# Post-norm attention and int8 linear layer on one core: the order of the last batch's requests, of the seam between batches, and of the splits of v and of the tokens

## The chip, the cores and the metric

The kernel runs on one core of one Trainium2 chip. The metric is the time of one execution on the device in microseconds (us); the time before is the median of three runs. A profile of one execution gives the times of instructions, from the start of its span.

## The reference

X has 4 batches of 1024 tokens with 512 features. With `q = X Wq` (16 heads of 64), `k = X Wk` and `v = X Wv` (8 heads of 64, each for two heads of q), and rotary embedding on q and k:

```
att = softmax(causal(50 * tanh(q k^T / 16 / 50)))
x   = layernorm(X + (att v) Wo)
q8, s = per-token int8 of x          # s = max(absmax, 1e-7) / 127, q8 = clip(round(x / s))
f   = float16((q8 @ weight^T) * s * w_scale + bias)
out = layernorm(x + f)
```

## The kernel before

Every float32 product is made of three products of rounded parts: high x high, high x low, low x high. ScalarE makes a high part by copying into the rounded type, VectorE or GpSimd (POOL) makes the low part by subtraction. The five engines each have an instruction list of their own, written out by hand, and wait for each other through semaphores. All loads, and the stores of intermediate results, are asked for by the queue SP in one order; the output stores are asked for by ScalarE's queue.

**A batch** (`b`) has 4 units (`u`), each for two heads of k and four of q, and a unit has 18 steps (`s`). Step `g = 18 u + s` treats one tile of 128 x 1024 scores:

- TensorE makes the scores (`score`), and three steps later (`LAG`) weighs v with the probabilities (`weigh`).
- ScalarE makes tanh (`cap`, the squashing) and exp (`exponent`). POOL sets the part over the diagonal to zero in the steps that have one (`mask`, one select or two). VectorE makes high and low parts (`probs_of`, which waits for the mask; `low_done` lets `weigh` go).
- ScalarE copies finished sums (`keep_sums`), and SP stores them to `y_scratch` (`put_sums`). The last row of the sums holds the softmax denominators.

**Beside the scores** a unit makes q and k of the next one, in three chunks (`x` = 0 for k, 1 and 2 for the halves of q). A chunk is 24 products of TensorE in three slices of 8 (`project`), a rotation on VectorE (`rope_read`, for k four operations of 1024 columns), a rounding on ScalarE (`round_rope`), a low part on VectorE (`rope_low`), and a spreading into `qk` by transfers (`put`: 4 for k, 8 for a half of q). `turns` says at which steps of the unit these run: its result for unit 3 is the list of steps moved by 2, 1 and 1. The chunks of unit 3 belong to the next batch, whose tokens are split in four parts (`split_x`, on ScalarE and VectorE) at the steps that `part_at` names. They are also what SP's loads of w_v, the weights of v, wait for.

**After the steps** TensorE makes v for the next batch (`project_v`), beside the inverses of the denominators. SP loads a group's denominators (`load_div`), VectorE inverts them (`invert`), SP stores the inverses (`store_inverse`) and loads them as rows (`load_rows`), TensorE spreads the rows over the partitions (`spread_rows`), and VectorE scales y with them (`scale_y`), which `load_y` has loaded. `round_y` and `split_y` (ScalarE, POOL) make its parts.

**Then come the 8 row tiles** (`t`) of 128 tokens: `project_out` (24 products with Wo), `residual1` (waits for X in `x_in`), `inverse_std`, `shift_by` and `norm1` for the first norm, `find_scale` and `quantise`, `turn_q` (4 transposes) with its copy `keep_q`, `linear`, `rescale`, `residual2` (two additions on POOL: bias, then the row), `stats2`, `inverse_std`, `shift_by`, `norm2` and `store` for the second. `inverse_std` of a tile waits for the norm of the one before. The tiles pass through rings: `ffn_tile` lies in the same buffer as the probabilities, and `done_tile` puts the last two tiles' output into `x_in`.

**The seam** is the end of a batch's tiles, in which the next batch's first steps have begun: scores 0 and 1 are made between the last tiles, the squashings of 0, 1 and 2 stand between the last norms, and that of 3 waits until the last norm is done, since tiles 6 and 7 lie in the buffer that it writes. In the last batch nothing follows, and the tiles run without work beside them.

**The start** makes v 0 to 7, the tables and the three chunks of unit 0. `round_v` and `split_v` make the high and low part of a tile of v; the first projection of unit 1 waits for all low parts of v and for `proj_read`.

## Time and profile before

| | |
|---|---|
| median of 3 runs | 1356.7 us (1356.2 to 1359.26) |
| the profiled execution | 1350.54 us |
| its span, first to last instruction | 1348.8 us |
| mean granted TensorE clock | 0.983 of full |
| TensorE busy | 1277.5 us, 95% |
| VectorE busy | 1041.9 us, 77% |
| ScalarE busy | 898.6 us, 67% |
| POOL busy | 392.6 us, 29% |

The span is measured within the profiled execution, whose own time lies 1.7 us above it. A batch takes about 327 us, so what is seen in batch 1 comes again in the next one some 327 us later. PE is TensorE, DVE is VectorE, ACT is ScalarE, and SPq is the request queue. L724 is line 724 of the kernel. A wait for several semaphores is put down to the one that came last, and "issue" means that the profile shows no releaser.

### The profile page before, as it was taken

How to read it: one execution, taken by the hardware profiler on the slowest of the kernel's cores; microseconds unless marked ns; L12 is line 12 of the kernel's file. 1: busy time of each engine (PE TensorE's matmuls, PEld its weight loads, DVE VectorE, ACT ScalarE, POOL GpSimd, SP SyncE). 2: the span in 40 equal slices, each digit the busy share in tenths (PEclk: the TensorE clock that was granted, in tenths of full speed). 3: DMA queues.
4: the chain of work that ended last, by engine and by line, in shares of the span. 5: the costliest groups of instructions: out<-in, count | busy, mean ns of one | idle time of the engine just before them, and what ended most of it. 6: DMA issues, size and time to landing. Idle time of an engine off the chain costs nothing.

```text
span 1348.8 us, 17012 instructions
## 1 busy us (share of the span) xinstructions
PE 1277.5 (95%) x5840; PEld 940.1 (70%) x5840; DVE 1041.9 (77%) x1300; ACT 898.6 (67%) x1017; POOL 392.6 (29%) x454
## 2 busy tenths in 40 slices
PE   7899999999989999999998999999999899999795
PEld 5677776767757777677775777767776677777473
DVE  4598998874778888986579888888567888888565
ACT  4378778663667777865466867787346687779354
POOL 4232221112751121111383211121157211111266
PEclk9899999999999999999999999999999999999897
DMA  8784647394715364658632644548662445353641
GB/s 312 172 254 117 150 107 197 89 256 144 176 60 134 83 163 98 176 116 259 158 103 63 168 94 120 114 152 214 194 171 83 91 128 111 87 120 111 169 111 55
DMA packets 112403, 191.46 MB, mean 142 GB/s; under 512 B 19382, under 2 KB 65980, under 8 KB 104764
## 3 DMA queue, kind: packets, MB, share of 16 engines
q1 hardware_dynamic: 107708, 181.97, 51.4%
q10 hardware_dynamic: 4608, 8.39, 1.7%
q8 instruction: 47, 0.77, 0.2%
q14 instruction: 40, 0.33, 0.1%
HBM read 84.67 MB, written 38.54 MB: 91 GB/s over the span
## 4 chain that ended last, share of the span: by engine, by line
PE 84%; DVE 6%; issue 3%; ACT 2%; POOL 2%; DMA 1%; SPq 1%; ACTq 0%; POOLq 0%; DVEq 0%
PE ps L804 26%; PE ps L724 18%; PE ps L778 17%; PE ps L848 12%; PE ps L745 6%; PE ps L868 1%; DVE prob_hi L1221 1%; PE ps L824 1%; DVE xT L1162 1%; DMA y_scratch<-sums 1%; ACT probs L998 1%; POOL rstd L1445 1%; DVE stats L1301 1%; POOL f L1454 0%; PE ps L858 0%
## 5 line engine op out<-in xcount | busy, mean ns | idle before, releaser
L804 PE MATMUL ps<-prob_hi,v 128*65 128x512 f32 (+3 forms) x1280 | 412.6, 372 | 4.5 <-DVE prob_lo L1225 4.2
L998 ACT ACTIVATE probs<-ps 128x1024 f32<-128x1024 f32 x288 | 293.6, 1019 | 149.2 <-PE ps L778 146.2
L1225 DVE TENSOR_TENSOR prob_lo<-probs,prob_hi 128x1024 fp32r<-128x1024 f32 x288 | 363.9, 1264 | 9.9
L1430 POOL TENSOR_SCALAR_AFFINE_SELECT probs<-probs 128x256 f32<-128x256 f32 (+1 forms) x192 | 154.9, 814 | 724.1 <-ACT probs L1003 724.1
L778 PE MATMUL ps<-qk 128*128 128x512 f32 (+1 forms) x1280 | 315.3, 373 | 14.7 <-ACT probs L998 13.0
L1003 ACT ACTIVATE probs<-probs 128x1024 f32<-128x1024 f32 x288 | 305.7, 1061 | 9.8 <-ACT probs L1047 1.2
L724 PE MATMUL ps<-xT,w_ring 128*128 128x512 f32 x1152 | 289.9, 395 | 11.0 <-DVE xT L1162 6.1
L1221 DVE CAST prob_hi<-probs 128x1024 fp32r<-128x1024 f32 x288 | 212.6, 738 | 90.9 <-POOL probs L1430 53.4
L778 PEld LDWEIGHTS ps<-qk 128*128 128x128 f32 x1280 | 225.5, 189 | 74.3 <-ACT probs L998 15.6
L724 PEld LDWEIGHTS ps<-xT,w_ring 128*128 128x128 f32 x1152 | 217.1, 190 | 58.9 <-DVE xT L1162 7.4
L804 PE MATMUL ps<-prob_lo,v 128*65 128x512 f32 (+1 forms) x640 | 237.8, 372 | 0.0
L804 PEld LDWEIGHTS ps<-prob_hi,v 128*65 128x65 f32 (+1 forms) x1280 | 171.6, 135 | 94.2 <-DVE prob_lo L1225 8.9
L848 PE MATMUL ps<-wo,y_hi 128*128 128x512 f32 x512 | 132.4, 402 | 1.3 <-POOL y_lo L1436 1.3
L804 PEld LDWEIGHTS ps<-prob_lo,v 128*65 128x65 f32 x640 | 87.1, 136 | 50.1 <-issue 0.4
L848 PEld LDWEIGHTS ps<-wo,y_hi 128*128 128x128 f32 x512 | 95.7, 191 | 29.7 <-issue 9.1
L1019 ACT ACTIVATE sums<-ps 65x512 f32<-65x512 f32 x128 | 74.5, 582 | 59.7 <-PE ps L804 59.7
L745 PE MATMUL ps<-w_v,xT 128*128 128x512 f32 x384 | 93.5, 400 | 10.2 <-DVE w_v L1316 8.1
L1436 POOL TENSOR_TENSOR y_lo<-y_raw,y_hi 128x1024 fp32r<-128x1024 f32 x32 | 76.5, 2391 | 90.1 <-ACT y_hi L1027 89.7
L745 PEld LDWEIGHTS ps<-w_v,xT 128*128 128x128 f32 x384 | 72.7, 192 | 29.1 <-issue 12.0
L848 PE MATMUL ps<-wo,y_lo 128*128 128x512 f32 x256 | 67.8, 389 | 0.0
L981 ACT ACTIVATE work_r<-work 128x1024 fp32r<-128x1024 f32 x48 | 50.1, 1044 | 18.6 <-DVE work L1201 10.6
L1207 DVE TENSOR_TENSOR work_r<-work,work_r 128x1024 fp32r<-128x1024 f32 x48 | 58.5, 1219 | 2.8 <-ACT work_r L981 2.8
(86 smaller groups left out, 967.1 us busy)
## 6 DMA issues: line engine op xcount, KB each, us to landing
qk<-work_r SPq DMA_DIRECT2D x64, 512.0 KB, 8.8
qk<-work_r SPq DMA_DIRECT2D x256, 128.0 KB, 2.7
y_scratch<-sums SPq DMA_DIRECT2D x128, 130.0 KB
wo<-wo_scratch SPq DMA_DIRECT2D x8, 2048.0 KB, 7.9
y_raw<-y_scratch SPq DMA_DIRECT2D x64, 256.0 KB, 4.2
w_ring<-w_scratch SPq DMA_DIRECT2D x12, 1024.0 KB, 6.8
x_raw<-X_T SPq DMA_DIRECT2D x16, 512.0 KB, 6.2
x_in<-X SPq DMA_DIRECT2D x32, 256.0 KB, 4.1
```

The source lines that it names most:

```text
L724: mm = nc.tensor.matmul(ps[:, bank + n, :], w_ring[:, slot, w, k, :], xT[:, a, k, half * HT:(half + 1) * HT], start=(k == w == a == 0), st ...
L745: mm = nc.tensor.matmul(ps[:, v_bank(b, t), :], xT[:, a, k, t * P:(t + 1) * P], weights[:, w, k, :], start=(k == a == w == 0), stop=(k == ...
L778: mm = nc.tensor.matmul(scores[:, g % 2, col:col + REP * w].rearrange("p (h q) -> p h q", h=REP), qk[:, n % 2, i, 3 - part, keys], qk[:, n ...
L804: mm = nc.tensor.matmul(sums_ps[:, :, GQ - w:GQ], v[:, kt, v0:v0 + width], p[:, at, col:col + REP * w].rearrange("p (h q) -> p h q", h=REP ...
L848: mm = nc.tensor.matmul(bank, (y_lo[:, y_place(t), k, :] if a else y_hi[t % 2][:, k, :]), wo[:, w, k, :], start=(n == 0), stop=(n == 3 * K ...
L998: nc.scalar.activation(probs[:, prob_place(g), :], scores[:, g % 2, :], ACT.Tanh, scale=SCORE_SCALE / SOFTCAP).then_inc(capped, 1)
L1003: nc.scalar.activation(probs[:, prob_place(g), :], probs[:, prob_place(g), :], ACT.Exp, scale=SOFTCAP).then_inc(exped, 1)
L1019: nc.scalar.activation(sums[0:VJ, slot, :], ps[0:VJ, PV_BANK + c % 2, :], ACT.Copy).then_inc(sums_kept, 1)
L1221: nc.vector.tensor_copy(prob_hi[:, hi_place(g), :], probs[:, prob_place(g), :]).then_inc(rounded, 1)
L1225: nc.vector.tensor_tensor(prob_lo[:, prob_place(g), :], probs[:, prob_place(g), :], prob_hi[:, hi_place(g), :].bitcast(F32), ALU.subtract) ...
L1430: nc.gpsimd.affine_select(out=diag, in_=diag, compare_op=ALU.is_ge, fill=0.0, base=0, pattern=[[0, n], [1, P]], channel_multiplier=-1).the ...
L1436: nc.gpsimd.tensor_tensor(y_lo[:, y_place(t), :, :], y_raw[:, y_place(t), :, :], y_hi[t % 2][:, :, :].bitcast(F32), ALU.subtract).then_inc ...
```

## The change

- **Start.** v tiles 6 and 7 are rounded and split sooner: ScalarE rounds them ahead of the rounding of chunk 2, and VectorE splits tile 6 ahead of that chunk's rotation and tile 7 ahead of its low part. The first projection of unit 1 no longer waits for `proj_read`.
- **Chunks.** In unit 3 the chunks run 3, 2 and 2 steps later than listed, not 2, 1 and 1; in unit 0 of every batch but the first they run one step later; the third chunk's rounding, low part and spreading stand one step sooner in the lists (so in units 1 and 2 they come a step sooner). The last token split moves from step 0 to step 1 of unit 3.
- **Seam.** Tiles 6 and 7 lie in `x_in` from the rescaling on, so the squashing of score 3 waits only for the stores of tiles 3 and 4. ScalarE does the squashings and exponentials of scores 1 to 3 ahead of the norm of tile 7, which moves with its store behind step 4, and copies the last quantised tile ahead of the exponential of score 1. VectorE rescales tile 7 ahead of the statistics of tile 6, makes probabilities 1 ahead of tile 6's shift, and makes tile 7's shift behind probabilities 2.
- **Last batch.** Inverse 0 is made and stored one step sooner. y 2, then the denominators of group 2, then rows 2 are asked for ahead of the last sums, and rows 3 right behind them; X still comes after. The first `project_out` begins with the products of high parts. The last quantised tile is copied ahead of a norm and its store, and VectorE makes the second residual of the last tile.

```diff
         def ffn_tile(t):
-            return blocks[:, FFN_BLOCK[t % FRING], :]
-        def done_tile(t):
-            return x_in[:, t % XRING, :] if t >= NT - 2 else ffn_tile(t)
+            return x_in[:, t % XRING, :] if t >= NT - 2 else blocks[:, FFN_BLOCK[t % FRING], :]
-        def turns(u, *steps):
-            return tuple(s + (2, 1, 1)[x] for x, s in enumerate(steps)) if u == UB - 1 else steps
+        def turns(b, u, *steps):
+            return tuple(s + (3, 2, 2)[x] for x, s in enumerate(steps)) if u == UB - 1 else \
+                tuple(s + 1 for s in steps) if b >= 1 and u == 0 else steps
-            return {(2, 15): 0, (2, 16): 1, (2, 17): 2, (3, 0): 3}.get((u, s))
+            return {(2, 15): 0, (2, 16): 1, (2, 17): 2, (3, 1): 3}.get((u, s))
 # SP
-                        if at := chunk_at(b, u, s, turns(u, 6, 11, 15)):
+                        if at := chunk_at(b, u, s, turns(b, u, 6, 11, 14)):
                             put(sp, *at)
+                        if (b, u, s) == (B - 1, UB - 1, 16):
+                            store_inverse(b, 0)
                         if u == UB - 1 and s == 17:
-                            if b + 1 == B:
-                                store_inverse(b, 0)
                             load_div(b, 1)
...
                 put_sums(b, NKV - 1, G - 2)
-                load_div(b, 2)
-                put_sums(b, NKV - 1, G - 1)
-                load_div(b, 3)
-                load_y(b, 2)
+                if b + 1 < B:
+                    load_div(b, 2)
+                    put_sums(b, NKV - 1, G - 1)
+                    load_div(b, 3)
+                    load_y(b, 2)
+                else:
+                    load_y(b, 2)
+                    load_div(b, 2)
+                    load_rows(b, 2)
+                    put_sums(b, NKV - 1, G - 1)
+                    load_rows(b, 3)
+                    load_div(b, 3)
                 for t in range(XRING):
                     load_x(b, t)
-                load_rows(b, 2)
-                load_rows(b, 3)
+                if b + 1 < B:
+                    load_rows(b, 2)
+                    load_rows(b, 3)
 # TensorE
-                    if m > 0:
+                    if m > 1 or x > 0 and m > 0:
                         pe.wait_ge(proj_read, chunks_upto(m, x) - 1)
-                products.sort(key=lambda p: p[1] if t else p[2])
-                if lo == (2 * KO if t else 0):
+                products.sort(key=lambda p: p[1] if t else (p[2], p[1]))
+                if lo == (2 * KO if t else KO):
                     pe.wait_ge(y_lo_done, rows_upto(b, t))
 # ScalarE
                     if g == 3:
-                        act.wait_ge(normed, rows_upto(b - 1, NT - 1))
+                        for t in (NT - 5, NT - 4):
+                            act.wait_ge(out_stored[t % FRING], stores_upto(b - 1, t))
...
-            round_rope(0, 2)
             round_v(0, 6)
             round_v(0, 7)
+            round_rope(0, 2)
...
+                        if b >= 1 and g == 4:
+                            norm2(b - 1, NT - 1)
+                            store(b - 1, NT - 1)
...
                 if more:
                     cap(b + 1, 1)
-                norm2(b, NT - 3)
+                    norm2(b, NT - 3)
+                keep_q(b, NT - 1)
+                if not more:
+                    norm2(b, NT - 3)
                 store(b, NT - 3)
                 if more:
                     exponent(b + 1, 1)
-                keep_q(b, NT - 1)
+                    cap(b + 1, 2)
+                    exponent(b + 1, 2)
                 norm2(b, NT - 2)
                 store(b, NT - 2)
                 if more:
-                    cap(b + 1, 2)
-                    exponent(b + 1, 2)
-                norm2(b, NT - 1)
-                store(b, NT - 1)
+                    cap(b + 1, 3)
+                    exponent(b + 1, 3)
+                else:
+                    norm2(b, NT - 1)
+                    store(b, NT - 1)
 # VectorE
+            def residual2(b, t):
+                dve.wait_ge(scaled, rows_upto(b, t))
+                dve.wait_ge(bias_loaded, bias_upto(b))
+                dve.wait_ge(x2_done, rows_upto(b, t - 1))
+                nc.vector.tensor_tensor(f16[:, :], ffn_tile(t), bias[:, :], ALU.add).then_inc(biased, 1)
+                dve.wait_ge(biased, rows_upto(b, t))
+                nc.vector.tensor_tensor(ffn_tile(t), f16[:, :], row_tile(t), ALU.add).then_inc(x2_done, 1)
...
             split_v(0, 5)
+            split_v(0, 6)
             rope_read(0, 2)
+            split_v(0, 7)
             rope_low(0, 2)
-            split_v(0, 6)
-            split_v(0, 7)
...
-                        if (b, u, s) == (B - 1, UB - 1, 16):
+                        if (b, u, s) == (B - 1, UB - 1, 15):
                             invert(b, 0)
                         if g >= 1 and not at_end(b, u, s - 1):
                             probs_of(b, g - 1)
+                        if b >= 1 and g == 3:
+                            shift_by(b - 1, NT - 1, 1, rstd2, shift2)
...
                 shift_by(b, NT - 3, 1, rstd2, shift2)
                 if more:
                     probs_of(b + 1, 0)
-                stats2(b, NT - 2)
+                if not more:
+                    stats2(b, NT - 2)
                 rescale(b, NT - 1)
+                if more:
+                    stats2(b, NT - 2)
+                else:
+                    residual2(b, NT - 1)
+                if more:
+                    probs_of(b + 1, 1)
                 shift_by(b, NT - 2, 1, rstd2, shift2)
-                if more:
-                    probs_of(b + 1, 1)
                 stats2(b, NT - 1)
-                shift_by(b, NT - 1, 1, rstd2, shift2)
+                if not more:
+                    shift_by(b, NT - 1, 1, rstd2, shift2)
 # POOL
                 residual2(b, NT - 2)
+                if b + 1 < B:
+                    mask(b + 1, 1)
                 inverse_std(b, NT - 2, 1, mv2, veps2, rstd2, normed)
                 if b + 1 < B:
-                    mask(b + 1, 1)
-                residual2(b, NT - 1)
+                    residual2(b, NT - 1)
                 inverse_std(b, NT - 1, 1, mv2, veps2, rstd2, normed)
```

The lists of the other engines for a chunk change alike: TensorE `turns(b, u, 0, 5, 9)`, VectorE's rotation `(b, u, 3, 8, 12)`, ScalarE's rounding `(b, u, 5, 10, 14)` becomes `(b, u, 5, 10, 13)`, VectorE's low part `(6, 11, 15)` becomes `(6, 11, 14)`. `mask` of score 1 does nothing, since that tile has no diagonal.

## Rows read from the trace of the kernel before

**Rows 1.** Waits of TensorE over the span: us in total, times, longest.

```profile
PE ps L778 <- ACT probs L998: 13.0, 6, 2.8
```

**Rows 2.** Timeline at the start: start, us, engine, line, out<-in, count, idle before.

```profile
54.98 0.68 DVE L1201 TENSOR_TENSOR work<-work 128x512 f32<-128x512 f32 x1
...
57.93 1.28 DVE L1167 TENSOR_TENSOR v<-ps,v 128x512 fp32r<-128x512 f32 x2
58.04 5.81 SPq L457 DMA_DIRECT2D qk<-work_r  x8
...
59.31 3.75 PE L724 MATMUL ps<-xT,w_ring 128*128 128x512 f32 x8 [4.39 <-issue]
...
66.25 1.07 PE L778 MATMUL ps<-qk 128*128 128x512 f32 x4
```

**Rows 3.** Chain that ended last, in order of time: start, us, what.

```profile
64.56 1.85 PE ps L724 x8
...
1238.56 1.39 PE ps L804 x6
1239.94 0.92 PE ps L778 x4
```

**Rows 4.** The page's transfer requests: count, KB each, median us to landing.

```profile
qk<-work_r SPq DMA_DIRECT2D x256, 128.0 KB, 2.7
...
result<-probs ACTq DMA_DIRECT2D x24, 256.0 KB, 2.3
```

**Rows 5.** Timelines around three waits: seam one, unit 3, seam two.

```profile
294.93 2.96 PE L745 MATMUL ps<-w_v,xT 128*128 128x512 f32 x12 [1.00 <-issue]
...
564.59 1.06 ACT L1003 ACTIVATE probs<-probs 128x1024 f32<-128x1024 f32 x1
...
567.73 2.11 PE L724 MATMUL ps<-xT,w_ring 128*128 128x512 f32 x8 [2.03 <-DVE xT L1162]
...
621.65 2.90 PE L745 MATMUL ps<-w_v,xT 128*128 128x512 f32 x12
```

**Rows 6.** The w_v requests ahead of seam two: issue times, landing.

```profile
L557 SPq DMA_DIRECT2D w_v<-wv_scratch x2: 442/442/443, 614.5 to 615.0; - x2
...
DMA to landing us min/median/max: 4.6/5.5/6.4
```

**Rows 7.** Timeline of seam one.

```profile
393.25 2.06 DVE L1225 TENSOR_TENSOR prob_lo<-probs,prob_hi 128x1024 fp32r<-128x1024 f32 x1
...
397.11 0.41 POOL L1430 TENSOR_SCALAR_AFFINE_SELECT probs<-probs 128x256 f32<-128x256 f32 x1
...
397.36 1.23 DVE L1186 TENSOR_TENSOR work<-ps,cosT 128x1024 f32<-128x1024 f32 x1
...
405.02 1.23 DVE L1225 TENSOR_TENSOR prob_lo<-probs,prob_hi 128x1024 fp32r<-128x1024 f32 x1
...
408.42 0.39 PE L804 MATMUL ps<-prob_hi,v 128*65 128x512 f32 x1
```

**Rows 8.** Timeline of the last batch's first tiles.

```profile
1267.17 0.32 SPq L487 DMA_DIRECT2D div<-y_scratch  x1
...
1271.19 1.08 SPq L472 DMA_DIRECT2D x_in<-X  x2
...
1275.37 0.69 DVE L1257 TENSOR_TENSOR probs<-ps,x_in 128x512 f32<-128x512 f32 x1 [5.72 <-DMA x_in<-X]
...
1276.67 1.19 PE L824 MATMUL ps<-rows,spread 4*128 4x512 f32 x2 [6.88 <-DMA rows<-r_scratch]
...
1281.35 0.72 ACT L1043 ACTIVATE q<-probs,round_down 128x512 bf16<-128x512 f32 x1
...
1286.63 3.94 PE L848 MATMUL ps<-wo,y_hi 128*128 128x512 f32 x16
```

**Rows 9.** Timeline of the end.

```profile
1339.90 0.75 DVE L1293 SCALAR_TENSOR_TENSOR probs<-ps,in_scale,w_scale 128x512 f32<-128x512 f32 x1 [0.57 <-PE ps L868]
...
1343.26 0.69 DVE L1301 BATCH_NORM_STATS2 stats<-probs 128x6 f32<-128x512 f32 x1 [2.49 <-POOL probs L1456]
```

More of the change, by code:

```diff
@@ L916, in _ @@
                         spread_rows(b, t + 1)
[L917 to L918 removed]
+                    for third in range(3):
+                        project_out(b, t, third * KO, (third + 1) * KO)
                     if t >= 2:
```

20 lines of the change are left out of this document (9 added, 11 removed).

## The prediction

> **What bounds the kernel now.** I read the page first, then the waits of TensorE, then the timeline around each wait, and the transfer queue where a wait ended on a transfer. TensorE is busy for nearly the whole span (the table above), so time can only be won where it stands idle or runs at the low clock. Its longest waits are for ScalarE's squashing at the three seams between batches, 13.0 us [rows 1]; the others fall at the start, before unit 3, in the last batch and at the end, and are taken one by one below. Inside the units it hardly waits. So I take the edits place by place, and ask each time which wait ends last afterwards.
>
> **Start: v split sooner.** The first projection of unit 1 starts at 59.31 after 4.39 us of idling [rows 2]. By the code it waits for all eight low parts of v. VectorE makes the last two from 57.93, 0.64 us each, because ScalarE rounds v 6 and 7 only after a rotation result that VectorE finishes at 54.98 + 0.68 = 55.66 [rows 2]. With the new order v 6 fits into VectorE's wait ahead of that rotation, and v 7 runs at 55.7 to 56.35. The projection may start at 56.4, 2.9 us sooner. What is late next is the second half of q: its eight requests run from 58.04 for 5.81 us, which does not move, since it needs the rotation's rounding; the score at 66.25 needs four of them. The fourth is issued at 58.04 + 3 x 0.73 = 60.2 and lands 2.7 us later, 62.9 [rows 2, 4]. That leaves room for 66.25 - 62.9 = 3.3 us, so the 2.9 holds. Bounds: 1.5 (requests landing later, as TensorE's idling moves there) and 3.3. I take 2.9 won.
>
> **Token splits and shifted chunks.** In each of the first three batches the first chunk of unit 3 waits 2.03 us, until 567.73 in batch 1, for the last token split [rows 5]. The split moves one step later, the chunk too. A step without projection is one score and one weighing, 1.39 + 0.92 = 2.3 us of TensorE [rows 3]. On ScalarE the exponential of unit 3's first step, done at 564.59 + 1.06 = 565.65 [rows 5], no longer stands behind the split and ends about 0.9 us sooner. Its mask is two selects of some 0.4 to 0.5 us, as the one of 0.41 [rows 7], and VectorE then has 2.0 us of probabilities and 1.2 us of split (a subtraction as wide as the 1.23 of rows 7). Exponential done 564.75, mask 565.9, probabilities 567.9, split 569.15. Without the shift TensorE would have started the same chunk after the same work at 567.73 + 2.3 = 570.0. Won: 0.8 per batch, 2.4 in all. Bounds: 0 (the mask slowed to twice its time by VectorE beside it) and the 2.03 x 3 = 6.1 of the waits.
>
> The same shift costs at the end of unit 3. There the queue asks for the second half of w_v right behind the requests of the middle chunk, which now come one step later. In the first seam TensorE already waits 1.00 us at 294.93 for v's first product. In the second the requests went at 614.5 and 615.0 and the later landed after 6.4 us, at 621.4, against a start of 621.65 [rows 5, 6]: no slack. A whole step is 2.3 us, but the sums of group 0 (0.6 us of queue) now go ahead of the chunk's requests, and VectorE does the chunk's low half before the next rotation and not behind it; I take 1.1. That is 1.1 lost in seam one, 1.1 - 0.25 = 0.85 in seam two, and I count nothing for seam three, where v's product started without a wait too (the 0.85 there is in the bounds): 2.0 lost. Bounds: 0 and 2.3 x 3 = 6.9. The other chunk edits (last third rounded a step sooner; unit 0 a step later) lie under TensorE's full stretches; without that cover each costs at most one rounding, about 1 us.
>
> **The seam.** The squashings of scores 1 to 3 go ahead of the last norms, so the 13.0 us of waits for them [rows 1] go. But VectorE is late next. In the old order it starts the rotation at 397.36, and ends the low half of probabilities 3 at 405.02 + 1.23 = 406.25, with almost no gap. TensorE weighs them at 408.42 [rows 7]. The rotation is four operations of 1.23, so it ended at 402.3, and a pair of probabilities takes (406.25 - 402.3) / 2 = 2.0. In the new order VectorE first does probabilities 2. Their mask ran at 397.11 to 397.52 behind POOL's last inverse deviation; POOL's order keeps that, and the statistics of tile 7 that it needs still come behind probabilities 1. So: mask 397.5, probabilities 2 to 399.5, rotation to 404.4, probabilities 3 to 406.4. TensorE has one slice of projection (1.85 us [rows 3]) less ahead of weighing 3, since unit 0's middle chunk is a step later: like for like it got there at 408.42 - 1.85 = 406.57. New against old, 406.4 to 406.57: nothing won. The waits for squashings turn into waits for probabilities and for the rotation. Bounds: 1.9 us either way per seam, about that pair, which the ordering may put outside or inside the chain. I take 0, since both sides of the sum are made of rows.
>
> Here a rule weighs against the change. Beside POOL's additions the low half at 393.25 took 2.06 us against 1.23 [rows 7]: the two engines slow each other. The Trainium skill, SBUF — State Buffer, section Who interferes with whom, says that VectorE with two inputs in SBUF and GpSimd contend, and that the one that starts first holds the shared ports for its whole instruction. The trace agrees that they contend; what holding would do here is rival (b).
>
> **Last batch.** TensorE idles 6.88 us until 1276.67 for rows 2. They were asked for behind y 2 and two tiles of X, and those behind a second pair of transfers for the sums. Now y 2, the inverses and the rows follow the first pair, which lands by 1267.17 [rows 8]; the rows' requests go at about 1267.6. Only y 2 is ahead of them, so they land at about 1270, and the second product block runs from 1271 to 1276.7. The next wait is then the first quantised tile. Its residual started at 1275.37, after 5.72 us of waiting for X, and it was complete at 1281.35 + 0.72 = 1282.07, 6.7 later [rows 8]. X is still asked for last, at about 1270.8. At 1271.19, behind y, it took 4.2 us [rows 8]; a store of the same size with nothing ahead takes 2.3 [rows 4]; I take 3.0, so 1273.8, 1.5 sooner, and the tile is ready at 1280.6. TensorE idles 3.9 us for it and comes back at the low clock, as at 59.31, where eight products after 4.39 us of idling took 3.75 against 1.85 us [rows 2, 3]: 1.9 us more, or 2.2 with the transposes ahead. The third block, at 1286.63 before [rows 8], starts at 1280.6 + 1.0 = 1281.6 behind turning and spreading: 5.0 us sooner, less 2.2: 2.8 won. Bounds: 1.5 (X hardly sooner) and 5.0 (clock kept). Inverses 0 gain little: their store now waits for the queue's four y requests, 0.25 us sooner than before. The first product's new order lets it start sooner, but the rows of tile 2 end that stretch.
>
> **Tail.** ScalarE copied the last quantised tile behind a norm and its store; it now comes ahead of them, about 1 us sooner. But the rescaling, at 1339.90 with 0.57 us of idling ahead, can move up only by these 0.57, as the statistics of tile 6 stand ahead. VectorE then adds bias and row itself: 2 x 0.69 (as the addition at 1275.37 [rows 8]) plus about 0.3 for waits and one shift, 1.7, where POOL's two took from 1340.65 to 1343.26, 2.6 [rows 9]. Won 0.55 + 0.9 = 1.45. Bounds: 0.6 and 2.
>
> **Sum.** -2.9 - 2.4 + 2.0 + 0 - 2.8 - 1.45 = -7.5 us. The profiled execution took 1350.54, so 1343.0 for the same; the median of the timed runs is 1356.7, 6.2 above it, and I set the difference against that: 1349.2. No change by measurement means within 0.2%, 2.7 us.
>
> **Rivals.** (a) The seams do give: VectorE's chain shortens by the 1.9 us each, or TensorE keeps its clock in the last batch. For it: VectorE has idle time there beside POOL. Against it: 406.25 is reached with hardly a gap. Gain 7.5 + 5.7 = 13.2 from the seams alone: 1343.5.
>
> (b) The ports decide. Probabilities 1 run against POOL's additions for tile 7; if POOL is held for both of VectorE's operations, 1.9 us per seam, its mask and all behind it are that much late: -7.5 + 5.8 = -1.7, 1355: no change. For it 2.06 against 1.23 [rows 7]; against it, the same pair met before. The rule of the first starter, in the Trainium skill, SBUF — State Buffer, section Who interferes with whom, would give just this if VectorE starts first.
>
> (c) Slower: the new knot on ScalarE. Squashing 2 now waits for the store of tile 5 and stands ahead of norm 6, which POOL's last deviation and so mask 2 wait for. Squashing and exponential take 2.1 us; with the store landing in the usual 2.3 us [rows 4] they end, as I count the order, some 3 us before norm 6 could start anyway, since its shift stands behind probabilities 1, whose low half ended at 395.31 before [rows 7]. It makes the kernel slower by over 0.2% from (7.5 + 2.7) / 3 = 3.4 us per seam beyond those 3, a landing of 8.7 us. The longest of the rows is 6.4 [rows 6]. Reached, it would give 1360.
>
> (d) The moves do not do what they say: the rows still land behind y and X, and w_v costs its full 6.9. Then -7.5 + 1.3 + 4.9 = -1.3: 1355.4.
>
> **How the numbers follow.** Forecast 0.56, (a) 0.22, (b) 0.08, (d) 0.08, (c) 0.06. The forecast's own range, from its bounds taken half together, is 1345 to 1353.5. With (a), half of (b) and (d), 8 in 10: 1342.5 to 1355.5. Faster: the forecast nearly whole and (a), with a little of the others, 0.83; same 0.11; slower 0.06.
>
> **What would show it.** Right: unit 1's first projection near 56.4; the chunk wait of unit 3 under 1.7 us; waits for ScalarE's squashings nearly gone and waits for VectorE's probabilities or rotation in their place; v's first product in seams one and two waiting about 2 and 0.8 us; rows 2 landing near 1270 on the old clock, with a wait for the quantised tile behind the second block; the end 1.4 us shorter behind the last product block. Wrong: seams shorter by over 1 us each, or TensorE at full clock after the wait in the last batch, would make it faster than I say; waits for w_v over 3 us, or a landing of tile 5's store that shows in squashing 2, slower.

## The result, and the profile after

The change makes the kernel slower: 1362.5 us (median of 6 runs, 1360.2 to 1363.8) against 1356.5 (6 runs beside them), ratio 1.0049 with a 95% interval of 1.0029 to 1.0069, 4 to 9 us. The prediction was 1349.2, faster.

The profiled execution took 1363.67 us, its span is 1361.9, and the granted clock 0.982 as before. The spans differ by 13.1 us and the medians by 6: the profiled execution of before lies 6 us under its median, this one 1 us above. So the traces tell where time goes, and the timed ratios how much.

Waits of TensorE over the span after: us in total, times, longest.

```profile
PE ps L813 <- DVE prob_lo L1243: 22.2, 24, 3.0
PE ps L867 <- ACT q L1053: 9.1, 5, 5.1
...
PE ps L787 <- ACT probs L1008: 5.6, 4, 1.4
PE ps L754 <- issue: 4.9, 3, 2.4
PE ps L733 <- DVE xT L1180: 4.4, 3, 1.5
PE ps L787 <- DMA qk<-work_r: 2.8, 1, 2.8
...
PE ps L833 <- DMA rows<-r_scratch: 1.6, 1, 1.6
```

The same view of the kernel before, for VectorE's low parts of probabilities:

```profile
PE ps L804 <- DVE prob_lo L1225: 4.2, 7, 0.8
```

The 13.0 us for squashings [rows 1] are 5.6 now, but three waits stand there that were small or absent: those low parts (22.2, before 4.2), q's transfer at the start (2.8, before none), and v's first product (L754, "issue": 4.9, before 1.0).

The start, TensorE's timeline:

```profile
56.59 2.09 PE L733 MATMUL ps<-xT,w_ring 128*128 128x512 f32 x8 [1.43 <-issue]
...
64.24 2.06 PE L787 MATMUL ps<-qk 128*128 128x512 f32 x4 [2.84 <-DMA qk<-work_r]
66.10 2.76 PE L733 MATMUL ps<-xT,w_ring 128*128 128x512 f32 x8
```

The projection came 2.7 us sooner, as said. This time TensorE kept the clock behind its wait (eight products in 2.09 us, against 3.75 [rows 2]), so it came to the score at 61.40 already. It waited 2.84 us for q, until 64.24 and not 62.9, and came back at the low clock: four products of the score took 2.06 us, against 1.07 [rows 2]. At the start of unit 1 (116 us) 0.3 us of the lead was left.

Unit 3 of batch 1, which answers to the 2.03 us wait of [rows 5]: POOL's selects in the kernel before (L1430), then, in the changed one, the same selects, the last split and the chunk.

```profile
565.82 2.35 POOL L1430 TENSOR_SCALAR_AFFINE_SELECT probs<-probs 128x256 f32<-128x256 f32 x2 [2.43 <-ACT probs L1003]
...
569.26 1.95 POOL L1465 TENSOR_SCALAR_AFFINE_SELECT probs<-probs 128x256 f32<-128x256 f32 x2 [1.84 <-ACT probs L1013]
...
573.12 1.22 DVE L1180 TENSOR_TENSOR xT<-x_raw,xT 128x1024 fp32r<-128x1024 f32 x1
...
574.39 2.11 PE L733 MATMUL ps<-xT,w_ring 128*128 128x512 f32 x8 [1.46 <-DVE xT L1180]
```

The end of unit 3, batch 0, on the queue and on ScalarE, and v's first product behind it:

```profile
268.53 7.42 SPq L450 DMA_DIRECT2D qk<-work_r  x4
275.99 1.95 SPq L650 DMA_DIRECT2D wo<-wo_scratch  x1
277.98 3.01 SPq L569 DMA_DIRECT2D y_scratch<-sums  x2
283.23 6.85 SPq L457 DMA_DIRECT2D qk<-work_r  x8
290.18 0.54 SPq L487 DMA_DIRECT2D div<-y_scratch  x1
290.82 0.87 SPq L557 DMA_DIRECT2D w_v<-wv_scratch  x2
...
289.90 0.59 ACT L1029 ACTIVATE sums<-ps 65x512 f32<-65x512 f32 x1 [2.67 <-DMA y_scratch<-sums]
...
297.29 0.94 PE L754 MATMUL ps<-w_v,xT 128*128 128x512 f32 x3 [0.20 <-issue]
...
629.57 4.29 PE L754 MATMUL ps<-w_v,xT 128*128 128x512 f32 x12 [2.26 <-issue]
...
963.43 2.97 PE L754 MATMUL ps<-w_v,xT 128*128 128x512 f32 x12 [2.44 <-issue]
```

The last two lines are v's first twelve products at the ends of batches 1 and 2. At the end of batch 0 the first starts 2.4 us later than before (294.93). w_v's second half was asked for at 290.82, where before it was at 287.16: it stands behind the middle chunk's eight requests, which start a step later, and now behind the denominators' request too, which keeps its fixed step 14. Beside this, ScalarE waits 2.67 us to copy sums: the buffer's last store, asked for right behind wo's 2 MB, took until then to land. In the trace's own chain of what ended last, batch 0 goes through that store:

```profile
277.98 11.84 DMA y_scratch<-sums
```

So TensorE waits only 0.20 us for w_v there; ahead of seams two and three it waits 2.26 and 2.44 us (1.00, 0 and 0 before). Behind the 2.26 the clock fell too: v's first twelve products took 4.29 us, against 2.90 [rows 5], and behind the 2.44 it did not (2.97).

Seam one, VectorE and TensorE (L1319 statistics, L1239 and L1243 probabilities, L1204 rotation):

```profile
398.48 0.69 DVE L1319 BATCH_NORM_STATS2 stats<-x_in 128x6 f32<-128x512 f32 x1 [2.29 <-POOL x_in L1491]
...
400.81 0.69 DVE L1239 CAST prob_hi<-probs 128x1024 fp32r<-128x1024 f32 x1 [1.31 <-POOL probs L1465]
...
402.81 1.22 DVE L1204 TENSOR_TENSOR work<-ps,cosT 128x1024 f32<-128x1024 f32 x1
...
402.82 0.69 PE L813 MATMUL ps<-prob_hi,v 128*65 128x512 f32 x1 [3.01 <-DVE prob_lo L1243]
...
410.12 0.45 PE L813 MATMUL ps<-prob_hi,v 128*65 128x512 f32 x1 [1.29 <-DVE prob_lo L1243]
```

TensorE waits 3.01 us in one piece and comes back at the low clock (0.69 us for a product that takes 0.39).

The last batch, queue, VectorE and TensorE; all is 16.5 us later than before:

```profile
1284.10 0.56 SPq L503 DMA_DIRECT2D rows<-r_scratch  x2
...
1287.54 1.84 SPq L472 DMA_DIRECT2D x_in<-X  x2
...
1286.45 0.73 PE L833 MATMUL ps<-rows,spread 4*128 4x512 f32 x2
...
1297.91 0.61 PE L867 MATMUL ps<-ident,q 128*128 128x128 bf16 x4 [5.09 <-ACT q L1053]
...
1299.60 5.67 PE L857 MATMUL ps<-wo,y_hi 128*128 128x512 f32 x16
...
1291.24 0.69 DVE L1275 TENSOR_TENSOR probs<-ps,x_in 128x512 f32<-128x512 f32 x1 [4.56 <-DMA x_in<-X]
```

Rows 2 are spread 6.7 us sooner than before, like for like (1286.45 - 16.5 against 1276.67 [rows 8]); X is only 0.6 us sooner (its residual at 1291.24 - 16.5 = 1274.7 against 1275.37). The new wait for the quantised tile, 5.09 us, costs the clock: the next 16 products take 5.67 us, against 3.94 [rows 8].

**Where the difference arises.** The start of ScalarE's squashing at the same step, after less before (us):

| batch, unit, step | before at | after | chunks_only | seam_only | seam_rotation |
|---|---|---|---|---|---|
| 0, 3, 14 | 284.26 | 0.85 | 0.58 | -0.15 | 0.96 |
| 1, 0, 0 | 374.65 | 2.42 | 3.23 | -1.41 | 1.24 |
| 1, 1, 0 | 444.14 | 3.46 | 3.05 | -0.01 | -1.02 |
| 1, 3, 14 | 612.14 | 4.42 | 3.71 | -0.22 | 0.59 |
| 2, 0, 0 | 701.28 | 9.61 | 9.20 | -0.21 | 0.57 |
| 2, 1, 0 | 770.80 | 10.56 | 8.98 | 1.10 | -1.74 |
| 2, 3, 14 | 938.79 | 11.53 | 10.11 | 1.11 | -1.50 |
| 3, 0, 0 | 1027.94 | 15.19 | 13.06 | 1.08 | -1.52 |
| 3, 1, 0 | 1097.71 | 15.90 | 12.61 | 2.02 | -4.10 |

From step 14 of unit 3 to the next batch's first squashing the change loses 1.6, 5.2 and 3.7 us; at the seams 1.0, 1.0 and 0.7. An unchanged stretch differs by up to 1.3 us between executions (seam_only -0.15 to -1.41), so one cell proves little. The three of one sign, and the same three in chunks_only, say more.

### The profile page after: what moved, and what is told of

Same layout as the page of the kernel before. It is cut to its first block, busy times and chain, and to the rows that moved or that the text cites. A ratio compares the mean times of both kernels' runs of the same rounds, so it can differ in the third digit from the quotient of the medians.

```text
span 1361.9 us, 17007 instructions
## 1 busy us (share of the span) xinstructions
PE 1286.8 (94%) x5840; PEld 939.5 (69%) x5840; DVE 1040.0 (76%) x1302; ACT 900.6 (66%) x1017; POOL 380.7 (28%) x452
## 4 chain that ended last, share of the span: by engine, by line
PE 71%; DVE 8%; DMA 5%; ACT 5%; issue 4%; POOL 4%; SPq 2%; POOLq 0%; DVEq 0%; ACTq 0%
PE ps L813 22%; PE ps L733 16%; PE ps L787 14%; PE ps L857 11%; PE ps L754 5%; DMA y_scratch<-sums 3%; DVE prob_hi L1239 2%; ACT probs L1013 2%; ACT probs L1008 2%; PE ps L833 1%; PE ps L877 1%; DMA x_raw<-X_T 1%; DVE prob_lo L1243 1%; DVE work_r L1225 1%; SPq L457 1%
## 5 line engine op out<-in xcount | busy, mean ns | idle before, releaser
L813 PE MATMUL ps<-prob_hi,v 128*65 128x512 f32 (+3 forms) x1280 | 415.9, 375 | 22.9 <-DVE prob_lo L1243 22.2
L1243 DVE TENSOR_TENSOR prob_lo<-probs,prob_hi 128x1024 fp32r<-128x1024 f32 x288 | 361.5, 1255 | 9.9
L1465 POOL TENSOR_SCALAR_AFFINE_SELECT probs<-probs 128x256 f32<-128x256 f32 (+1 forms) x192 | 141.5, 745 | 749.6 <-ACT probs L1013 749.6
L1239 DVE CAST prob_hi<-probs 128x1024 fp32r<-128x1024 f32 x288 | 207.6, 721 | 98.1 <-POOL probs L1465 51.2
L857 PE MATMUL ps<-wo,y_hi 128*128 128x512 f32 x512 | 129.0, 404 | 0.0
L754 PE MATMUL ps<-w_v,xT 128*128 128x512 f32 x384 | 95.0, 404 | 14.3 <-DVE w_v L1343 8.1
L754 PEld LDWEIGHTS ps<-w_v,xT 128*128 128x128 f32 x384 | 73.3, 194 | 34.2 <-issue 16.6
L1225 DVE TENSOR_TENSOR work_r<-work,work_r 128x1024 fp32r<-128x1024 f32 x48 | 62.5, 1301 | 2.2 <-ACT work_r L990 2.2
L857 PE MATMUL ps<-wo,y_lo 128*128 128x512 f32 x256 | 63.4, 390 | 0.0
```

Source lines behind the costliest of these rows:

```text
L754: mm = nc.tensor.matmul(ps[:, v_bank(b, t), :], xT[:, a, k, t * P:(t + 1) * P], weights[:, w, k, :], start=(k == a == w == 0), stop=(k == ...
L813: mm = nc.tensor.matmul(sums_ps[:, :, GQ - w:GQ], v[:, kt, v0:v0 + width], p[:, at, col:col + REP * w].rearrange("p (h q) -> p h q", h=REP ...
L857: mm = nc.tensor.matmul(bank, (y_lo[:, y_place(t), k, :] if a else y_hi[t % 2][:, k, :]), wo[:, w, k, :], start=(n == 0), stop=(n == 3 * K ...
L1225: nc.vector.tensor_tensor(work_r[:, place, 0, :], work[:, place, 0, :], work_r[:, place, 1, :].bitcast(F32), ALU.subtract).then_inc(rope_l ...
L1239: nc.vector.tensor_copy(prob_hi[:, hi_place(g), :], probs[:, prob_place(g), :]).then_inc(rounded, 1)
L1243: nc.vector.tensor_tensor(prob_lo[:, prob_place(g), :], probs[:, prob_place(g), :], prob_hi[:, hi_place(g), :].bitcast(F32), ALU.subtract) ...
```

## The experiments

All are compared with the kernel before, run beside them (its median 1352.1 to 1354.0). Each is the kernel before with the named edit, unless it says otherwise. The code in the fences is shortened to the calls that move.

**chunks_only**: the new lists of chunks, in all units, and the new step of the last token split.

```diff
-(2, 1, 1)[x] ... if u == UB - 1 else steps
+(3, 2, 2)[x] ... if u == UB - 1 else s + 1 if b >= 1 and u == 0
-(5, 10, 14), (6, 11, 15); (3, 0): 3
+(5, 10, 13), (6, 11, 14); (3, 1): 3
```

> The kernel before with the chunk lists and the last token split of the change alone. Theory Q (the end of unit 3 is crowded by the shift: the sums of group (7,0), the middle chunk's requests and the second half of w_v come behind each other on the queue, and ScalarE's copy of the next sums waits for the landing of the earlier ones): this part loses about 2 us ahead of the first seam and 3.6 us ahead of each of the next two, 8 to 10 us in all, 1.006 to 1.0075 of the kernel before; v's first product of seam one comes at about 297 where before it came at 294.93. Rival T (the loss is the seam's new order and the chunk edits are free): within 2 us of the kernel before, v's first product at 295 or earlier.

Measured 1.0081 (1.0060 to 1.0103). It is the larger loss, a little above Q's range. By the table 2.7, 5.5 and 3.0 us go in unit 3's end, none in the seams. On ScalarE and the queue:

```profile
290.40 0.59 ACT L1021 ACTIVATE sums<-ps 65x512 f32<-65x512 f32 x1 [3.44 <-DMA y_scratch<-sums]
...
291.18 1.06 SPq L559 DMA_DIRECT2D w_v<-wv_scratch  x2
...
298.13 1.17 PE L747 MATMUL ps<-w_v,xT 128*128 128x512 f32 x4 [0.55 <-issue]
```

**seam_only**: the edits listed under Seam.

```diff
-    norm2(7); store(7)  ...  g == 3: wait normed
+    cap, exponent(2); ... cap, exponent(3)  ...  g == 4: norm2(7); store(7)
```

> The kernel before with the seam's new order alone (tiles 6 and 7 in x_in, squashings of scores 1 to 3 ahead of the last norm, probabilities 1 ahead of tile 6's shift). Theory Q: the waits for squashings turn into waits for probabilities and cost 1.2 us more per seam, 3.6 us in all, 1.0025; without the chunk edits nothing is lost ahead of a seam. Rival T: the seam is where the time goes, 8 us or more, 1.006. Rival U (the seam's order wins once the chunks are not moved, since TensorE has its slice of unit 0's chunk as cover again): 2 to 6 us faster, 0.9955 to 0.9985.

Measured 1.0024 (1.0012 to 1.0036), as Q said. VectorE, TensorE, and a window of seam one (its length, the busy times of TensorE, its weight loads, VectorE, ScalarE and POOL, then the granted clock, DMA share and GB/s):

```profile
394.64 0.69 DVE L1311 BATCH_NORM_STATS2 stats<-x_in 128x6 f32<-128x512 f32 x1 [2.29 <-POOL x_in L1472]
...
399.63 3.75 PE L724 MATMUL ps<-xT,w_ring 128*128 128x512 f32 x8 [3.66 <-DVE work L1199]
...
400.00:404.00 4.00, 4.00 (x10) 2.76 (x10) 3.93 (x6) 0.93 (x2) 0.00 (x0) 0.50 0.02 4
```

TensorE starts this projection at 399.63, before at 401.31. Of these 1.7 us, 1.4 were there before the seam began (the table's -1.41). The eight products then take 3.75 us and not 2.09, at 0.50 in the window, the low level, and the next slice starts at 406.60 in both kernels.

**last_tail**: requests and inverse 0 of the last batch, the first product's order, the tail.

```diff
-load_div 2; put_sums; load_div 3; load_y 2; load_x 0, 1; load_rows 2, 3
+load_y 2; load_div 2; load_rows 2; put_sums; load_rows 3; load_div 3; load_x 0, 1
```

> The kernel before with the last batch's requests, its inverse 0, the order of the first output product and the tail alone. All theories: from the last batch's first spreading of the rows to the last output product 1.8 us less, behind it 1.6 us less, as in the changed kernel: -3.4 us, 0.9975. If the first output product's new order, which all batches have, costs or wins at the seams, it shows as a difference ahead of the last batch; I expect none over 0.5 us.

Measured 0.9979 (0.9967 to 0.9992), 2.8 us for last batch and tail together (1.1 to 4.5).

```profile
1281.79 0.61 PE L869 MATMUL ps<-ident,q 128*128 128x128 bf16 x4 [5.36 <-ACT q L1054]
...
1283.48 6.62 PE L859 MATMUL ps<-wo,y_hi 128*128 128x512 f32 x16
```

The third block starts 3.2 us sooner than before (1286.63 [rows 8]) and takes 2.7 us more at the low clock, so some 0.5 us are left of the last batch's gain in this trace. In the changed kernel, like for like, it starts 3.7 us sooner and takes 1.7 more: 1.9 us.

**start_only**: the edits listed under Start.

> The kernel before with the start's edits alone. From the trace of the changed kernel: the first projection of unit 1 near 56.6 where before it came at 59.31, then 2.8 us of waiting for the half of q and a stretch at the low clock; at 115 us no lead is left. So 0 us, 0.9985 to 1.0015. Rival: the lead of 2.7 us is kept where the other edits are absent, 0.998.

Measured 0.9992 (0.9978 to 1.0005): no proven gain. Its trace disagrees with the expectation: a lead of 2.95 us stands at the start of unit 1, 2.7 at that of unit 3.

```profile
56.30 3.49 PE L726 MATMUL ps<-xT,w_ring 128*128 128x512 f32 x8 [1.45 <-issue]
```

Here the low clock fell on this projection, behind a wait of 1.45 us, as it did in the kernel before. So TensorE came to the score later, waited only 0.62 us for q, at 63.17, and ran at full clock from there. The changed kernel kept the clock on the projection (2.09 us behind a wait of 1.43), waited 2.84 us for q and lost the clock behind that. Whether the lead holds differs between executions.

**chunks_wo_late**: chunks_only with the request for wo's first half at step 15, not 11.

> chunks_only (1.0081) with the request for wo's first half, 2 MB, moved from step 11 of unit 3 to step 15, behind those of w_v. In chunks_only four spreadings of the first chunk, 2 MB, end at 275.8 and wo follows at once; wo takes 14.3 us to land (9.8 before), a store of sums asked for right behind it at 277.66 lands only near 290.4, and ScalarE's next copy of sums waits 3.44 us for it. Theory Q (these two big transfers back to back are the loss): without wo ahead the store lands in some 3 to 5 us, the copy does not wait, and 2.5 to 4 us per batch come back: 1.000 to 1.003. Rival V (the loss is the later landing of w_v, as the prediction had it, or VectorE's work at the end of unit 3): at least 1.006 stays.

Measured 1.0158 (1.0132 to 1.0184): far from theory Q's range, and within V's "at least 1.006", but not for V's reason. ScalarE's wait was gone, but TensorE waited for rows behind wo instead, 19.6 us in five waits (6.5 in two in chunks_only). Not a fair test of Q, since it moved 2 MB ahead of the rows' chain.

**first_chunk_only** and **other_chunks_only**: `(3, 1, 1)` with the split, and `(2, 2, 2)` without it.

> The kernel before with only the first chunk of unit 3 a step later (3, 1, 1 in place of 2, 1, 1) and the last token split with it. Theory Q: its spreading comes right ahead of wo's request, so the sums' store lands late and ScalarE waits: most of the loss, 1.004 to 1.007, less some gain from the token split. Rival V (w_v behind the middle chunk): within 0.1% of the kernel before or 1 to 2 us faster by the shorter wait for the last token split.

> The kernel before with only the second and third chunk of unit 3 a step later (2, 2, 2 in place of 2, 1, 1). Theory Q: the first chunk's spreading keeps its place, wo lands in some 10 us, the copy of sums does not wait; what stays is w_v, 1 to 2 us per seam less whatever is hidden: 1.001 to 1.003. Rival V: 1.006 or more.

Measured 1.0180 (1.0155 to 1.0206, four runs) and 1.0040 (1.0021 to 1.0060), both above what I gave. The two do not add up to chunks_only (1.0081): moved alone, the first chunk comes a step closer to the second, and VectorE waits for that (below). Without the first chunk's shift wo landed in 9.7 us (14.3 in chunks_only), ScalarE did not wait, and v's product still waited for w_v, asked for at 289.1. With the first chunk's shift alone, ScalarE waited 6.87 us for the sums, and VectorE's next rotation 6.04 us for the first chunk's transfers to leave `work_r`:

```profile
287.25 1.23 DVE L1205 TENSOR_TENSOR work<-ps,cosT 128x1024 f32<-128x1024 f32 x1 [6.04 <-DMA qk<-work_r]
```

**wo_behind_sums**: chunks_only with wo asked for at step 12, behind the store that ScalarE waits for.

> chunks_only (1.0081) with wo's first half asked for behind the store of sums that ScalarE waits for, and not ahead of it; everything else, the 4 spreadings of the first chunk directly ahead of it too, stays. In chunks_wo_late, where wo came behind w_v, ScalarE's wait for the store was gone (step 15 of unit 3 at +1.43 on the clock of before, against +4.13 in chunks_only), but TensorE then waited 19.6 us for rows behind wo. Theory Q: here the store is ahead of wo, so ScalarE's copy does not wait (chunks_only: 3.44 us), wo lands as late as in chunks_only, some 14 us, and rows wait no longer than before; left are w_v's 1 to 2 us per seam and the units' 1 us: 1.002 to 1.005. Rival W (the two big transfers hurt whatever stands behind them, the spreading of the middle chunk and w_v too): 1.006 or more, with the wait moved to another transfer.

Measured 1.0088 (1.0066 to 1.0110): theory Q is wrong as the cause, and rival W's range holds. ScalarE copies the sums at 286.04 without a wait, and TensorE waits for w_v instead, till nearly the same time:

```profile
286.04 0.58 ACT L1021 ACTIVATE sums<-ps 65x512 f32<-65x512 f32 x1
...
289.95 0.94 SPq L559 DMA_DIRECT2D w_v<-wv_scratch  x2
...
296.90 4.58 PE L747 MATMUL ps<-w_v,xT 128*128 128x512 f32 x12 [3.21 <-issue]
```

In chunks_only the two waits overlapped, and the profile showed the one that hid the other. From step 14 of unit 3 to the next batch's first squashing this trace loses 3.9, 0.8 and 4.4 us (chunks_only 2.7, 5.5 and 3.0). The large losses stand where v's first twelve products ran at the low clock behind the wait: they took 4.58, 2.99 and 4.42 us here and 3.01, 4.26 and 2.98 in chunks_only. In both, v's product starts 6.95 us after the first w_v request (298.13 - 291.18, 296.90 - 289.95).

**div_behind** and **wv_ahead**: wo_behind_sums with the denominators' request behind w_v; and, separately, with w_v ahead of the middle chunk's eight requests.

```diff
 put(sp, middle chunk)            +load_wv 1, 2
-load_div(b, 0)                    put(sp, middle chunk)
 load_wv 1, 2                      load_div(b, 0)
+load_div(b, 0)                   -load_wv 1, 2
```

> wo_behind_sums (1.0088) with the denominators' request of unit 3's step 14 behind w_v's second half, where it stood in the kernel before, and not ahead of it. In wo_behind_sums TensorE starts v's first product 6.95 us after the first of the two w_v requests (289.95, 296.90), as in chunks_only (291.18, 298.13), and the spreading of the middle chunk ends at 288.61. Theory R (the time at which the queue comes to w_v sets the seam's begin): w_v is asked for about 0.9 us sooner after a given start of the chunk's spreading, 3 us in all: 1.0065. Rival: the landing of w_v does not follow its request but the backlog of transfers, 1.0085 stays.

> wo_behind_sums (1.0088) with w_v's second half asked for ahead of the spreading of unit 3's middle chunk, which takes the queue some 6.5 us, and not behind it. Theory R: w_v is asked for near 282.5 instead of 289.95, the wait for it (3.2, 0.4 and 2.7 us at the three seams, all others in the same place) is gone and v's first product starts as soon as the last weighing of unit 3 is done: 3 us per seam back, 1.001 to 1.003. Rival: the middle chunk or the sums, now behind w_v, are waited for instead: 1.006 or more.

Measured 1.0057 (1.0038 to 1.0077) and 1.0079 (1.0059 to 1.0099). The one request of denominators ahead of w_v is worth some 3 to 4 us in this kernel (0.31% between the ratios; 3.0 us between the traces), but the intervals overlap, so it is likely and not proven. Nor is it the wait that shrank (TensorE's waits for w_v are 6.3 us in wo_behind_sums and 5.8 in div_behind): in div_behind v's first twelve products took 3.00, 3.00 and 2.99 us, and the two low stretches that are gone are 3.0 us. With w_v asked for at 281.45 its wait was gone at all seams, but no gain is proven, as the rival said: the next chain ended the stretch, denominators, inverses and rows:

```profile
309.08 0.70 PE L829 MATMUL ps<-rows,spread 4*128 4x512 f32 x2 [1.96 <-DMA rows<-r_scratch]
```

**after_unit3_undone**: the changed kernel with `(2, 1, 1)` and `(3, 0): 3` as before.

> The changed kernel with the lists of unit 3 and the last token split as they were before; all else of the change stays, the later chunks of unit 0 and the earlier third chunk too. Theory Q (the loss is unit 3's shift): the 8 to 12 us of unit 3 come back and about 1 us per seam stays lost, about 1 us for the third chunk's earlier place, less 3.4 us for the last batch and tail: 0.998 to 1.0005 of the kernel before. If the seam's order and the other chunk edits were the larger part of the loss, it stays over 1.002.

Measured 1.0001 (0.9989 to 1.0012), against 1.0049 with the shift: the intervals do not meet. Unit 3's lists are worth 0.5%, 6.5 us, all of the loss against the kernel before. The rest of the change comes out even (within 1.6 us), where the prediction had it win 7.15.

**seam_rotation**: seam_only with two instructions moved.

```diff
 # VectorE
-probs_of(1); shift_by(6); stats2(7); | rope_read; probs_of(2)
+probs_of(1); shift_by(6); | rope_read; stats2(7); probs_of(2)
 # POOL
-residual2(7); inverse_std(7); mask(2)
+residual2(7); mask(2); inverse_std(7)
```

> seam_only (1.0024) with the statistics of tile 7 behind unit 0's first rotation on VectorE and the last inverse deviation behind the mask of score 2 on POOL. In seam_only VectorE waits 2.29 us for POOL's sum of tile 7 with that rotation behind it; TensorE waits 3.66 us for the rotation and runs the next eight products at the low clock, 3.75 us where 1.98 is usual. Theory M (the seam's order would win, but one long wait in place of several short ones costs the clock): the rotation starts 2.2 us sooner, TensorE waits about 1.5 us and keeps its clock, 2 to 4 us per seam won against seam_only: 0.994 to 0.999 of the kernel before. Rival B (VectorE's total work in the seam is the bound, whatever its order): 1.0 to 1.0025.

Measured 0.9935 (0.9915 to 0.9954), 8.8 us faster than before, 12 than seam_only:

```profile
394.96 1.23 DVE L1196 TENSOR_TENSOR work<-ps,cosT 128x1024 f32<-128x1024 f32 x1
...
398.92 2.08 PE L724 MATMUL ps<-xT,w_ring 128*128 128x512 f32 x8 [0.28 <-DVE work L1199]
...
402.77 0.44 PE L804 MATMUL ps<-prob_hi,v 128*65 128x512 f32 x1 [1.78 <-DVE prob_lo L1235]
...
400.00:404.00 4.00, 2.22 (x11) 1.23 (x10) 3.37 (x6) 1.53 (x2) 2.49 (x3) 1.00 0.08 23
```

VectorE's wait for POOL is filled with the rotation, TensorE's one wait of 3.66 becomes 0.28 and 1.78, and the clock stays at 1.00. From the score ahead of these waits to the first weighing behind the second slice TensorE takes 13.6 us in seam_only (394.77 to 408.41) and 9.5 here (397.42 to 406.96). Seam two of this same trace shows how much of the 4.1 us is the clock:

```profile
724.86 3.58 PE L724 MATMUL ps<-xT,w_ring 128*128 128x512 f32 x8 [0.29 <-DVE work L1199]
...
728.72 0.45 PE L804 MATMUL ps<-prob_hi,v 128*65 128x512 f32 x1 [0.28 <-DVE prob_lo L1235]
```

There the clock fell on the projection in spite of the short waits, and yet the weighing comes 3.86 us behind the projection's start, as in seam one (3.85): VectorE's probabilities set that time. They are done 7.7 us behind the score in seam_only (402.50 - 394.77) and 5.3 here (402.72 - 397.42), so VectorE's order accounts for 2.4 of the 4.1 us, and the low clock for the other 1.7 (0.6 ahead of the weighing, 1.1 behind it). Theory M gave a range just above the ratio and is half right: the clock is the smaller part. B falls.

**x_first**: last_tail with X's first tile behind rows 2; the second tile stays, since it lies in the buffer of the last sums.

> last_tail (0.9979) with X's first tile in the last batch asked for right behind rows 2, ahead of the last sums, rows 3 and the last denominators: at 1268.3 where it was 1271.14. In last_tail TensorE waits 5.36 us for the first quantised tile, until 1281.79, and the next 16 products take 6.62 us at the low clock where 3.94 is usual. Theory X (the first quantised tile waits for X, and the one long wait costs the clock): the first residual runs 2 to 3 us sooner, TensorE waits some 3 us, and with the clock kept 4 to 5 us are won against last_tail, without it 2 to 3: 0.994 to 0.997 of the kernel before. Rival: X lands no sooner, since what stands ahead of it in the transfer engines is the same: 0.9975 to 0.9985.

Measured 0.9950 (0.9933 to 0.9967). The wait for the quantised tile fell from 5.36 to 3.73 us; less than X's lead of about 4 us, since VectorE's inverse 3 now stood ahead of the first shift and waited 1.74 us for its buffer's store. The clock fell still.

**together**: start_only, seam_rotation, last_tail, x_first.

> The parts that won, together: start_only, seam_rotation, last_tail and x_first; no chunk edits. If the parts add up: 0.9935 for the seam, 0.0021 less for last batch and tail, 0.0008 less for the start and 0.001 to 0.004 less for X: 0.986 to 0.990. If they overlap (the last batch has no seam and the start has none, so they should not): 0.992.

Measured 0.9887 (0.9870 to 0.9905), 1337.9 against 1354.0 us: faster than both kernels, and the parts add up. **together_wv**, the same with w_v ahead of the middle chunk:

> together (0.9887) with w_v's second half asked for ahead of the spreading of unit 3's middle chunk. Theory R: together waits 2.0 us without a named releaser and 0.8 us at v's first products; what of it is w_v goes, 1 to 3 us in all: 0.9865 to 0.988. Rival: the middle chunk's spreading, 0.9 us later, or the transfers behind it cost as much: 0.9885 to 0.990.

Measured 0.9930 (0.9906 to 0.9954), worse, as its rival said and more: waits for rows again (6.8 us in five, together 1.8 in two).

## Why the prediction was wrong, point by point

The forecast was 7.5 us faster and the result is 6 us slower, 13.5 us apart. Unit 3 is half of it: -0.4 (the split and w_v) was predicted and +6.5 measured. The rest of the change is the other half: -7.15 was predicted and about 0 measured.

- **w_v, the step that failed.** "A whole step is 2.3 us ... I take 1.1": 1.1, 0.85 and 0 were taken, 2.0 in all, with 6.9 as bound. The unit 3 edits cost 6.5 us net, and TensorE's waits for w_v grew by 3.9 (from 1.00 to 0.20 + 2.26 + 2.44). I named the sums of group 0 as the only thing to change places on the queue. But the denominators' request stands at a fixed step, and the shift moved w_v behind it; w_v was asked for 3.7 us later (290.82 against 287.16). Of these, 0.85 had been lost before that step (the table), 2.3 are the step and 0.5 are slower requests of the chunk; the denominators' request took the place that the sums had left, so none of the 1.2 us of relief came. By div_behind this one place is likely worth 3 to 4 us. Not in the sum at all was the clock: behind the wait of 2.26 us the products took 1.4 us more. How the rest divides stays open: at unit 3's end three chains end close to each other (ScalarE's sums, w_v, the rows), and each time one was eased the next ended last. The order of SP's list around every moved item had to be written out; it was not.
- **The first chunk's transfers**, not in the sum at all. Its 2 MB now come right ahead of wo's 2 MB; wo lands after 13.7 us in the changed kernel, 9.8 before, and the store behind it late. It added a wait on ScalarE, which by wo_behind_sums costs little by itself. The Trainium skill, DMA: Bandwidth & Descriptors, section Queues, rings and completion order, says that on each transfer engine descriptors are consumed in ring order and that a semaphore's increment lands only after that engine's earlier writes. The trace agrees: the chain has 11.84 us for the store asked for at 277.98, which so landed at 289.82, right behind wo (275.99 + 13.7).
- **Token split**: 0.8 per batch predicted, about 0 measured. The first slice came at 574.39, 6.66 later than before; less a step of 2.3 that is 4.36, and the unit had begun 4.25 late. The exponential was sooner as said, but POOL's two selects took 1.95 us beside VectorE's probabilities, not 0.8 to 1.0: the text's own lower bound. The trace of before had them at 2.35 us, at 565.82; the 0.41 of [rows 7] ran away from VectorE's probabilities.
- **Other chunk edits**: put at nothing. 0.16 us at each third chunk of units 1 and 2, some 1.3 us in the trace.
- **Seam**: predicted 0, 1.9 either way; measured 0.7 to 1.0 per seam in the changed kernel, 3.2 in all by seam_only. VectorE was rightly named as next, but was later than said: on the old clock (less 2.4) the mask of score 2 ran at 398.0 (said 397.5), its probabilities ended at 400.4 (399.5), and TensorE weighed tile 3 at 407.7 (406.57). Missing were VectorE's wait of 1.31 us for that mask, and the clock. Rival (a), that the seams give 5.7 us, fell with the order as written; with seam_rotation's they gave more (8.8 by the ratio, 7.2 by the table). Rival (b), the ports, was right in kind and wrong in place: the additions for tile 7 did not meet probabilities 1, but the inverse deviation of tile 6 did. Its second operation on POOL took 1.54 us, the next one's 0.55 (both of the changed kernel):

```profile
394.40 1.54 POOL L1480 TENSOR_TENSOR rstd<-veps,minus_half 128x1 f32<-128x1 f32 x1
...
399.85 0.55 POOL L1480 TENSOR_TENSOR rstd<-veps,minus_half 128x1 f32<-128x1 f32 x1
```

  With its first operation (0.61 against 0.19) that is 1.4 us of the 2.29 for which VectorE then waits for POOL's sum. The rule that the prediction cites from the Trainium skill, SBUF — State Buffer, section Who interferes with whom, fits an operation on one column that is held so long; that a port is what holds it, no run here shows.
- **Start**: "leaves room for 3.3, so the 2.9 holds" failed in the changed kernel: q landed for the score at 64.24, 1.3 us later than the median landing gave. And the room was reckoned from a score at 66.25, behind a projection at the low clock. With that clock kept, TensorE was there 2.84 us ahead of q. The traces show 0.3 to 3 us won, by where the low clock falls; the timed runs of start_only prove no gain.
- **Last batch**: the mechanism was right. Like for like (last_tail) rows 2 were spread at 1270.06, said 1270; TensorE waited 5.36 us, said 3.9; the restart cost 2.7, said 2.2. X was mis-sized: 0.24 us sooner, not 1.5. So 2.8 was predicted, and 0.5 (last_tail) and 1.9 (changed kernel) measured in the traces.
- **Tail**: 1.45 predicted, 1.6 measured (from the start of the last eight output products to the end 22.06 before, 20.46 after).
- Rival (c), the knot on ScalarE, gave the right sign for the wrong reason: squashing 2 never waited for tile 5's store. Rival (d) had w_v's full 6.9, near the 6.5 that unit 3 cost net, but kept the split's gain; its other half, the rows late, was false.

## What to carry to other kernels

When a step of one engine moves, write out anew the request queue's whole order around it: an item with a fixed place that is overtaken can cost more than the step. A wait that the profile names may hide another that ends at the same time; take the first away before you believe its size. Fill the wait of the engine that feeds TensorE with work whose result TensorE needs next: it shortens the wait, and a long wait also costs the clock behind it.

## What the runs showed of the hardware

- TensorE came back at the low clock (1.2 GHz, half speed in the rows) from single waits of 3.66, 3.01, 5.09 and 2.84 us. Behind shorter waits it went either way at the same place. Behind v's wait for w_v the clock fell within the twelve products after 2.26 and 2.33 us (the changed kernel and chunks_only) and not after 2.44 and 2.87 (the changed kernel and div_behind). At the start it stayed full behind 1.43 us in the changed kernel and fell behind 1.45 in start_only, stayed behind 2.15 in together and fell behind 2.30 in after_unit3_undone. In seam_rotation it stayed behind 0.28 in seam one and fell behind 0.29 in seam two. The Trainium skill, Perfetto Trace Analysis, section Matmul Optimizations, says that the engine scales power with utilization and that matmuls should run back to back. The traces agree in that the low level came behind waits; they show the clock, not the power.
- A low clock costs only where TensorE is what the time waits for: 8 products in 3.58 us and in 2.08 us led to the same start of the next weighing (3.86 and 3.85 us behind them, seam_rotation).
- At the end of unit 3 of batch 0 wo's 2 MB landed after 9.7 and 9.8 us (other_chunks_only, before) and after 13.5 to 14.3 with the first chunk's 2 MB right ahead (first_chunk_only, the changed kernel, chunks_only).
- POOL is slowed beside VectorE: two selects of 128 x 256 took 1.95 and 2.35 us beside VectorE's probabilities, where one took 0.41 away from them [rows 7].
